# Hybrid attention / routed FFN / Mamba kernel: convolution taps, softplus and first scan step in another order, one positive part on VectorE

## The reference, cut to what matters

```python
xz = x @ w_in
xm, z = jnp.split(xz, 2, axis=-1)                  # 256 channels each
xc = conv(xm, w_conv) + b_conv                     # 4 taps in time, per channel
xm = silu(xc)
proj = xm @ w_xproj                                # dt (64), B (16), C (16)
delta = softplus(dt @ w_dt + b_dt)
deltaA = exp(delta[..., None] * A)                 # 16 states per channel
deltaBu = delta[..., None] * Bc[:, :, None, :] * xm[..., None]
h = deltaA * h + deltaBu                           # scan over the tokens of a sequence
y = (h * Cc).sum(states) + xm * Dp
out = (y * silu(z)) @ w_out
```

## Time and profile before

| | us |
|---|---|
| median of 3 runs | 940.75 (940.24 to 942.75) |
| the profiled execution's own time | 941.38 |
| its span, from the first to the last instruction | 939.5 |
| DVE busy | 711.1 (76% of the span) |
| PE busy | 643.7 (69%) |
| ACT busy | 538.4 (57%) |
| POOL busy | 449.6 (48%) |

### The profile page before, as it was taken

One profiled execution on the slowest core, in us unless ns is written; L12 is line 12 of the kernel. 1 busy time (PEld: TensorE's weight loads), 2 busy tenths in 40 slices (PEclk: granted clock), 3 DMA queues, 4 the chain that ended last, 5 costly groups with the idle time before them and its releaser, 6 DMA issues.

```text
span 939.5 us, 13919 instructions
## 1 busy us (share of the span) xinstructions
PE 643.7 (69%) x4284; PEld 513.3 (55%) x4285; DVE 711.1 (76%) x1785; ACT 538.4 (57%) x1116; POOL 449.6 (48%) x301
## 2 busy tenths in 40 slices
PE   4996116874898767778787887778799971159600
PEld 3775006862343367677676776677677760058600
DVE  6877883446754689999999999999988757845311
ACT  1562002232667989999999999999654620013200
POOL 3000005637400059898989899898710000047474
PEclk9998556996999869999999999999999995559955
DMA  8001101332100123332333233333500002014333
GB/s 203 7 1 53 38 0 43 100 76 54 36 1 6 28 57 104 102 100 101 101 100 104 97 104 95 100 101 101 169 1 1 1 26 64 0 31 109 80 97 81
DMA packets 61778, 62.79 MB, mean 67 GB/s; under 512 B 9079, under 2 KB 42682, under 8 KB 61722
## 3 DMA queue, kind: packets, MB, share of 16 engines
q1 hardware_dynamic: 57178, 52.77, 19.3%
q0 software_dynamic: 4544, 9.32, 4.6%
HBM read 50.40 MB, written 11.67 MB: 66 GB/s over the span
## 4 chain that ended last, share of the span: by engine, by line
DVE 31%; ACT 26%; PE 21%; POOL 11%; issue 8%; DMA 3%; DVEq 0%; POOLq 0%; SPq 0%; ACTq 0%
ACT work L775 12%; DVE work L1232 12%; POOL work L567 6%; POOL r_zs L572 5%; ACT wfold L747 4%; DVE work L985 4%; ACT dBuT L747 4%; PE bank L1678 3%; DMA work<-normed_rows,source 2%; PE bank L1666 1%; PE decay_ps L1666 1%; PE bank L1457 1%; PE decay_ps L1468 1%; PE decay_ps L1625 1%; PE decay_ps L1546 1%
## 5 line engine op out<-in xcount | busy, mean ns | idle before, releaser
L1232 DVE TENSOR_TENSOR_SCAN work<-work,decay_ps 128x1024 f32<-128x1024 f32 x128 | 290.5, 2270 | 1.9 <-PE decay_ps L1582 1.9
L583 POOL TENSOR_TENSOR work<-work,C_bc 128x1024 f32<-128x1024 f32 x86 | 204.5, 2378 | 110.2 <-DVE work L1232 109.7
L567 POOL DMA_INDIRECT work<-normed_rows,source x78 | 74.9, 961 | 297.0 <-DVE source L1085 271.9
L775 ACT ACTIVATE work<-r_delta,Aneg 128x510 f32<-128x510 f32 x256 | 170.1, 712 | 9.0 <-DVE work L1232 7.5
L1595 PE MATMUL bank<-ident,work 128*128 128x128 f32 x1024 | 133.6, 274 | 0.1
L1595 PEld LDWEIGHTS bank<-ident,work 128*128 128x128 f32 x1024 | 116.7, 142 | 0.3 <-POOL work L583 0.3
L583 POOL TENSOR_TENSOR work<-work,win_s 128x1024 f32<-128x1024 f32 x42 | 99.9, 2378 | 11.0 <-DVE work L1232 11.0
L1582 PE MATMUL decay_ps<-ident,wfold 128*128 128x128 f32 x512 | 70.5, 282 | 37.4 <-DVE wfold L1224 24.5
L1582 PE MATMUL decay_ps<-ident,dBuT 128*128 128x128 f32 x512 | 69.5, 280 | 34.5 <-DVE dBuT L1224 34.5
L1582 PEld LDWEIGHTS decay_ps<-ident,wfold 128*128 128x128 f32 x512 | 56.8, 144 | 50.1 <-ACT wfold L747 41.7
L747 ACT ACTIVATE wfold<-duT,B_T 128x256 f32<-128x256 f32 x192 | 82.8, 494 | 1.4 <-PE decay_ps L1582 1.4
(11 more groups left out here) (262 smaller groups left out, 1268.6 us busy)
## 6 DMA issues: line engine op xcount, KB each, us to landing
C_bc<-routed_out SPq DMA_DIRECT2D x86, 256.0 KB, 3.1
win_s<-routed_out SPq DMA_DIRECT2D x42, 256.0 KB, 3.1
routed_out<-work SPq DMA_DIRECT2D x26, 192.0 KB
normed_rows<-r_zs SPq DMA_DIRECT2D x2, 2048.0 KB, 9.4
X<-in_L_attn_a_input_data SPq DMA_DIRECT2D x4, 512.0 KB, 5.7
r_du<-in_L_ffn_W SPq DMA_DIRECT2D x2, 1024.0 KB, 6.7
r_du<-in_L_ffn_W SPq DMA_DIRECT2D x4, 512.0 KB, 8.3
out<-X SPq DMA_DIRECT2D x8, 256.0 KB, 2.4
```

The costliest lines, as they stand in the source:

```text
L567: pool.indirect_dma_start(out=xin[:, i % 2, s, :], out_offset=None, in_=normed_rows, in_offset=bass.IndirectOffsetOnAxis(ap=source[:, k:k ...
L583: pool.tensor_tensor(h[:, m % 4], h[:, m % 4], col(C_bc[m % 3]).broadcast_to([P, NB, G]), ALU.mult).then_inc(c_hC, 1)
L775: last = A(o, d, ACT.Exp, scale=Aneg[:, b, n:n + 1])
L1232: V.tensor_tensor_scan(h[:, m % 4].rearrange("p b t -> p (b t)"), decay[:, m % 2].rearrange("p b t -> p (b t)"), decay_ps[:, m % 2].rearra ...
```

## The change

Six things are different.

1. **Taps.** In the convolution, DVE takes the older taps of group g-4 ahead of `joined` of groups g and g+1, and those of group g-3 behind their `factors`, from g = 4 on; behind `factors` of groups 2 and 3 there are none. The taps of groups 4, 5 and 6 stand together at the end.
2. **Positive part.** ACT makes both absolute values (block 1 first, with a semaphore `m_abs`) and only the positive part of block 0. DVE makes that of block 1 from the same bank, as one instruction that adds the bias and takes the maximum with 0 (`second_relu`, semaphore `m_relu`).
3. **Waits.** `softened` waits for `m_abs`, `soft` and `to_raw` (for the banks), and the first two `turned_dBu`, wait for `m_relu`.
4. **B columns.** The copy of the B columns is taken out of `soft` into `kept_b`, which stands behind `second_relu`.
5. **First decay.** ACT makes the decay of step 0 ahead of `folded` of group 7, behind waits for delta of group 6 and for the zeroed columns.
6. **Last softplus.** DVE does `soft` of group 7 behind the first `scan`.

The last hunk below is PE's, in `to_raw`.

```diff
             def folded(g):
...
-                for b in range(NB):
-                    ch.step(A(ln_part[s][:, b], bank[4 + 2 * s + b], ACT.Abs, bias=bdt_s[:, b:b + 1]))
-                for b in range(NB):
-                    last = A(pos_part[s][:, b], bank[4 + 2 * s + b], ACT.Relu, bias=bdt_s[:, b:b + 1])
-                last.then_inc(m_raw, 1)
+                A(ln_part[s][:, 1], bank[5 + 2 * s], ACT.Abs, bias=bdt_s[:, 1:2]).then_inc(m_abs, 1)
+                ch.step(A(ln_part[s][:, 0], bank[4 + 2 * s], ACT.Abs, bias=bdt_s[:, 0:1]))
+                A(pos_part[s][:, 0], bank[4 + 2 * s], ACT.Relu, bias=bdt_s[:, 0:1]).then_inc(m_raw, 1)
...
+                act.wait_ge(m_abs, g + 1)
...
                 if g == NG - 2:
                     act.wait_ge(m_bt, 1)
                     scaled(0)
+                    act.wait_ge(m_delta, NG - 1)
+                    act.wait_ge(c_zero, 1)
+                    decayed(0)
             act.wait_ge(m_bt, NG)
-            act.wait_ge(m_delta, NG - 1)
-            act.wait_ge(c_zero, 1)
             for m in range(STEPS):
...
             for g in range(2, NG, 2):
+                if g > 2:
+                    later_taps(g - 4)
                 joined(g)
                 joined(g + 1)
                 factors(g, 2)
-                later_taps(g - 2)
-                later_taps(g - 1)
-            later_taps(NG - 2)
+                if g > 2:
+                    later_taps(g - 3)
+            for g in range(NG - 4, NG - 1):
+                later_taps(g)
...
+            def second_relu(g):
+                s = g % 2
+                dve.wait_ge(m_abs, g + 1)
+                V.tensor_scalar(pos_part[s][:, 1], bank[5 + 2 * s], bdt_s[:, 1:2], 0.0, ALU.add,
+                                ALU.max).then_inc(m_relu, 1)
...
             for g in range(1, NG):
                 projected(g)
+                second_relu(g - 1)
+                kept_b(g - 1)
                 soft(g - 1)
...
+            second_relu(NG - 1)
+            kept_b(NG - 1)
             ch.step(V.tensor_scalar(gate[:, :], rs, 1.0, None, ALU.add))
-            soft(NG - 1)
...
                 scan(m)
+                if m == 0:
+                    soft(NG - 1)
...
                 pe_.wait_ge(m_raw, g + 1)
+                if g > 1:
+                    pe_.wait_ge(m_relu, g - 1)
```

More of the change, by code:

```diff
@@ L342, in hybrid_kernel @@
         m_raw = sem("m_raw")
+        m_abs = sem("m_abs")
+        m_relu = sem("m_relu")
         m_soft = sem("m_soft")
@@ L753, in _, with decayed @@
             softened(0)
[L754 to L763, removed]
-            act.wait_ge(m_delta, NG - 1)
-            act.wait_ge(c_zero, 1)
-            for m in range(STEPS):
+            def decayed(m):
                 g, n = m // N, m % N
@@ L776, in _ @@
                 last.then_inc(c_decay, 1)
+            for g in range(1, NG):
+                folded(g)
+                softened(g)
+                if g >= NG - GT:
+                    if g < NG - 1:
+                        turned_du(0, g - (NG - GT))
+                if g == NG - 2:
+                    act.wait_ge(m_bt, 1)
+                    scaled(0)
+                    act.wait_ge(m_delta, NG - 1)
+                    act.wait_ge(c_zero, 1)
+                    decayed(0)
+            act.wait_ge(m_bt, NG)
+            for m in range(STEPS):
+                g, n = m // N, m % N
+                if m > 0:
+                    decayed(m)
                 if m + 1 < STEPS:
@@ L1198, in projected, with kept_b @@
                 V.tensor_copy(proj[0:PR, g % 2], bank[g % 2][0:PR, :]).then_inc(m_dt, 1)
-            def soft(g):
-                at = tokens_of(g)
+            def second_relu(g):
[3 more added lines that the diff above has]
+                                ALU.max).then_inc(m_relu, 1)
+            def kept_b(g):
                 dve.wait_ge(m_bt_ps, g + 1)
@@ L1206, in soft @@
                                   m_bt, 1)
+            def soft(g):
+                at = tokens_of(g)
+                dve.wait_ge(m_relu, g + 1)
                 dve.wait_ge(m_soft, g + 1)
@@ L1579, in turned_dBu @@
                     pe_.wait_ge(m_raw, NG + 1 + m)
+                    pe_.wait_ge(m_relu, NG - 1 + m)
                 for k in range(GT):
```

## The result

The changed kernel takes 937.62 us (median of 11 runs, 937.23 to 940.11) against 941.50 (940.03 to 944.92) for the kernel before, timed beside it on the same chip. The ratio is 0.9962 with a 95% interval of 0.9949 to 0.9975. The time lies at the upper end of the range, and not by any of the cases from which the range was made.

The account below looks back on a forecast made before the run. PE with two waits bounds the convolution, an ACT-DVE-PE loop the softplus, then a serial tail; DVE bounds the scan stage, which gains nothing. 3.1 + 2.3 + 0.4 = 5.8 us; 940.75 - 5.8 = 935.0 us, range 933.6 to 937.8.

Parts of the forecast that it names:

- the cases from which the range was made: Whole kernel: the forecast with its spread, Rival (2) below and Rival (4) above; 933.6 to 937.8 us.
- Taps: Convolution: PE's waits for normed rows go, five groups take 32.25 us instead of 35.33; gain 3.1 us.
- Rival (3): Convolution: taps gain nothing, PE waits for taps or ACT is late by other work; 938.0 us, chance 0.05.
- Positive part: Softplus loop: ACT loses 0.58 us per group, loop 9.2 instead of 9.80, DVE's new instruction covered; gain 2.3 us.
- Rival (4): Softplus: gains nothing because DVE or PE takes ACT's place on the loop; 937.6 us, chance 0.06.
- Tail: From group 6 done on DVE to the second scan: 11.1 us against 11.51; gain 0.4 us.
- its t: Tail: the time at which group 6 is done on DVE, with its last B columns; before at 327.11.
- delta of group 7 at t + 8.7: Tail: group 7's ln ends at about t + 5.4, hidden, as DVE needs it only at t + 8.7.
- What the prediction listed as a sign: Tail: delta of group 7 starts behind the first scan without a wait; no size given.
- The other sign: Scan stage: an ACT wait larger than now would make the prediction wrong; no size given.
- rival (1): Softplus: PE's clock falls to half three groups earlier, 10.2 us lost; 945.1 us, slower than before, chance 0.03.
- Rival (2): Tail: PE keeps full clock to the first product, 1.94 falls to about 1.0; 1.2 us more, 933.8, chance 0.06.

Follow-up runs that it names:

- experiment 2: The changed kernel with one wait more: POOL starts its first multiplication only when du of group 7 is done; 935.71 us.
- experiment 6: Parts alone in the kernel before: positive part 938.27 us; first decay and last softplus moved 941.51; taps 939.54, once more 940.13.
- experiment 4: The changed kernel with soft of group 7 split: delta behind the first scan, du behind the second; 935.49 us.
- experiment 5: The changed kernel with group 7's B columns and two scaled_last ahead of the last positive part: 935.81 us; with POOL also held until du is done, 934.56.

## Why the prediction was right and wrong

- **Taps: right.** 3.08 us for 3.1, all five groups at 6.45, no wait in PE's or ACT's place. Rival (3) is out.
- **Positive part: right in its mechanism, 0.3 too large.** The instruction costs 0.74 us (0.7 forecast) and ACT's chain is 0.58 shorter. But the loop fell by 0.51, to 9.29 instead of 9.2; the other places gained 0.5 each as well. The missing 0.07 stands between ln and delta: 311.14 - 309.89 = 1.25, against 304.82 - 303.64 = 1.18 in the earlier trace rows. Delta now waits for two semaphores where it waited for one. The traces point to this: the chain shows a piece of DVE's queue (DVEq) at L1229, the wait for `m_soft`, which the chain before does not have, and of the kernels with one part alone the one with the second wait has 1.25 too (321.84 - 320.59 at group 6), and the one without it 1.18 (325.02 - 323.84, the same group). No run took out this wait and nothing else. Rival (4) is out.
- **Tail: wrong, and this is the step that failed.** The term was "delta and du of group 7, 333.32 - 330.92 = 2.4" from the earlier trace rows. It measured 336.05 - 331.64 = 4.41 us. All other terms up to the first scan held: decay, absolute value, positive part, PE's turns and product add up to 6.57 us from the zeroed columns, where the forecast's terms make 6.4 (6.25 less 0.1, and the 0.26 by which the last B columns, its t, stood behind the zeroed columns in the kernel before). So of the 2.2 between the gain of 0.4 and the loss of 1.8, delta and du are 2.0. What failed in them is the overlap: the prediction let DVE work beside POOL at the price that it has beside an idle POOL, and the runs showed 3.25 us for `du` behind POOL's multiplication and 1.22 without it. The price of 2.4 came from a place where POOL was idle, ahead of the first scan, and was carried to a place behind it, where POOL is released at that very moment. With 1.22 for `du`, experiment 2 has a tail of 11.54 and a gain of 0.2 where 0.4 was forecast. (The prediction needs delta of group 7 at t + 8.7; its own terms make 8.45. Nothing hangs on it.)
- **What the prediction listed as a sign was there, and hid the loss.** Delta of group 7 did start behind the scan without a wait. The wait was inside the next instruction's duration. The other sign, an ACT wait in the scan stage larger than before, appeared as well (4.46 us ahead of the fourth decay), as a consequence: ACT waits for the second scan.
- **Clock: rival (1) is out** for this kernel. In its profile the granted clock was 1.00 up to 318 us, before up to 321, and fell in or just behind PE's idle time ahead of the last w_dt product, which took 3.65 us for 3.78. The dips of experiment 6 reach the same half clock, but cost no more than 1.5 us in the softplus where they were seen. That a shorter loop would rather hold the clock, the argument against this rival, is not borne out: dips were seen with the shorter loop too (experiments 2, 4 and 5). Rival (2) is out too: the first product took 1.94 as before.
- The sum would have been 3.1 + 2.0 - 1.8 = 3.3, and the time about 937.5 from the median given (938.2 from the 941.50 timed beside the change). That the range held the measured time is luck: its upper end came from rival (4), a softplus that gains nothing, and that is not what happened. None of the four rivals was a price that depends on the neighbour.

## What to carry to other kernels

A duration holds for the neighbours with which it was measured: when an instruction is moved, look at what the other engines run at its new place, VectorE and GpSimd above all, and price it from a row in which they run together, or by the sum of both as the upper end. Here the wait for the other engine showed as a longer instruction and not as idle time, so compare the instances of one line by their durations. If the two must meet, let the engine on the critical path start first (by its place in the order, by splitting the pair, or by a wait on the other engine), and don't queue ready work of the critical path behind a wait for the one late value.

## What the runs showed of the hardware

- A 128x1024 tensor_tensor of VectorE in fp32 with both inputs in SBUF took 1.20 to 1.23 us where GpSimd was idle or started behind it, and 3.25 to 3.27 behind a GpSimd multiplication of that size. The latter took 2.36 to 2.39 beside VectorE's scans and 3.23 to 3.26 behind such a tensor_tensor. A lead of 0.16 to 0.17 us decided who waited, in every run that had the two together.
- VectorE's scans, scalings and gate products, each with an input from PSUM, ran beside the same GpSimd multiplications all through the scan stage at 2271, 453 and 676 ns on average; with GpSimd idle the first scan took 2.29 us and the scalings ahead of it 0.47 to 0.48.
- A two-operation tensor_scalar of 128x512 from PSUM took 739 ns on average.
- TensorE's granted clock fell to half (0.50 in whole microseconds) for some 3 to 4 us in the softplus in some executions and not in others, at different places for one and the same kernel. PE was busy 2.83 of the 4 us ahead of the dip in the first execution of the taps alone, and 2.83 of the same 4 us in the kernel before, whose clock stayed at full.
